# Row groups by one-row DMAs on SyncE, a hand-over awaited by TensorE, ranges of 46 nodes

## The reference, cut to what matters

```python
nodes = x[edges]                                   # source's and destination's state, side by side
gates = ssp(edge_attr @ We1 + be1) @ We2 + be2     # ssp is softplus less log 2
gates = gates * (1 - sigmoid(5 * (distance - 3.5)))
h = ssp(nodes @ Wn1 + bn1) @ Wn2 + bn2
sums = zeros_like(x).at[dst].add(h * gates)
new = x + ssp(sums @ Ws1 + bs1) @ Ws2 + bs2
out = layernorm(x + new)
```

## Time and profile before

| | us |
|---|---|
| median of three runs (1990.34 to 1991.43) | 1991.15 |
| the profiled execution | 1991.78 |
| its span, first to last instruction | 1989.6 |
| share of the span busy: TensorE, weight load, VectorE, ScalarE, GpSimd | 88%, 67%, 64%, 74%, 75% |

### The profile page before, as it was taken

The page is one execution under the profiler, slowest core; times in us unless marked ns, Lnnn a source line. Parts: engine busy times, 40 slices in busy tenths (PEclk is TensorE's granted clock), DMA queues, the critical chain, the costliest instruction groups (busy, mean ns, idle before and its releaser), DMA issues.

```text
span 1989.6 us, 52758 instructions
## 1 busy us (share of the span) xinstructions
PE 1744.9 (88%) x16249; PEld 1331.2 (67%) x16249; DVE 1281.8 (64%) x3512; ACT 1470.9 (74%) x2586; POOL 1483.8 (75%) x1572
## 2 busy tenths in 40 slices
PE   4699999989889888899888998888998898888897
PEld 3477777777667666666666776666776666666666
DVE  4577777766655655656566666666666666666666
ACT  2478888877776777767677777777777777777776
POOL 7777777777777777777777777777777777777773
PEclk7799999998998999989999999999989999999999
DMA  5433333333333333333333333333333333333331
GB/s 120 118 89 96 93 95 93 91 93 77 90 74 69 73 70 73 75 69 73 70 76 72 74 77 77 75 74 80 73 75 75 77 75 75 75 77 75 75 76 38
DMA packets 256432, 157.78 MB, mean 79 GB/s; under 512 B 45401, under 2 KB 227046, under 8 KB 256366
## 3 DMA queue, kind: packets, MB, share of 16 engines
q1 hardware_dynamic: 202652, 104.94, 18.1%
q0 software_dynamic: 50048, 51.35, 15.6%
q10 hardware_dynamic: 3666, 0.68, 0.2%
HBM read 146.94 MB, written 9.87 MB: 79 GB/s over the span
## 4 chain that ended last, share of the span: by engine, by line
POOL 55%; issue 20%; PE 14%; ACT 3%; DVE 2%; DMA 2%; SPq 2%; ACTq 1%; DVEq 0%; POOLq 0%
POOL ga L459 55%; PE ps L623 4%; PE ps L636 3%; PE ps L640 2%; PE ps L585 1%; PE ps L575 1%; DMA ga<-in_x_dram,srcT 1%; DVE hid L1114 1%; SPq L340 1%; ACT lg L865 1%; PE ps L653 1%; ACT lg L860 1%; PE ps L662 1%; PE ps L577 1%; DVE hid L1118 1%
## 5 line engine op out<-in xcount | busy, mean ns | idle before, releaser
L459 POOL DMA_INDIRECT ga<-in_x_dram,srcT x1564 | 1482.8, 948 | 477.7 <-issue 472.4
L852 ACT ACTIVATE lg<-ps,bn1c 128x512 f32<-128x512 f32 x391 | 268.6, 687 | 374.9 <-PE ps L585 351.7
L636 PE MATMUL ps<-wn,hid 128*128 128x64 f32 x3128 | 446.6, 287 | 35.7 <-DVE hid L1118 31.0
L1114 DVE SCALAR_TENSOR_TENSOR hid<-ps,neg_b,lg 128x512 f32<-128x512 f32 x391 | 293.0, 749 | 264.5 <-ACT lg L865 253.0
L636 PEld LDWEIGHTS ps<-wn,hid 128*128 128x128 f32 x3128 | 391.8, 197 | 71.6 <-DVE hid L1118 48.5
L860 ACT ACTIVATE lg<-lg 128x768 f32<-128x768 f32 x391 | 335.6, 858 | 0.0
L865 ACT ACTIVATE lg<-lg 128x768 f32<-128x768 f32 x391 | 332.2, 850 | 0.0
L575 PE MATMUL ps<-ident,ea 128*128 128x128 f32 x782 | 173.6, 305 | 174.2 <-DMA ga<-in_x_dram,srcT 117.6
L844 ACT COPY xe<-ps 128x512 f32<-128x512 f32 x391 | 230.0, 588 | 104.9 <-PE ps L577 92.0
L623 PE MATMUL ps<-xe,wn 64*128 64x256 f32 x1564 | 293.1, 453 | 0.0
L640 PE MATMUL ps<-we,hid 128*128 128x128 f32 x1564 | 274.5, 301 | 0.0
(11 more groups left out here) (122 smaller groups left out, 1526.3 us busy)
## 6 DMA issues: line engine op xcount, KB each, us to landing
ea<-in_edge_attr_dram SPq DMA_DIRECT2D x195, 256.0 KB
ga<-in_x_dram,srcT POOLq DMA_INDIRECT x1564
bw<-b_tab SPq DMA_DIRECT2D x782, 32.0 KB
relb<-rel_tab SPq DMA_DIRECT2D x196, 64.0 KB
b_tab<-share SPq DMA_DIRECT2D x25, 250.0 KB
out_dram<-xs SPq DMA_DIRECT2D x25, 125.0 KB
xs<-in_x_dram SPq DMA_DIRECT2D x3, 750.0 KB
rows_i<-in_dst_dram SPq DMA_DIRECT2D x1, 768.0 KB
```

The source lines that it names most:

```text
L459: pool.indirect_dma_start(to[:, t % 2, t // 2, :], None, x, bass.IndirectOffsetOnAxis(ap=idx[:, t:t + 1], axis=0)).then_inc(done, 16)
L636: pe.matmul(hg[:, t * D:(t + 1) * D], hid[:, u % 2, t * P:(t + 1) * P], wn2[:, :], start=False, stop=False, skip_group_check=True)
L852: act.activation(lg[:, u % 2, 0:QUAD].rearrange("p (k e) -> p k e", k=2), z[:, :, 0:PAIR], ACT.Abs, bias=bn1c[:, 0:1])
L1114: dve.scalar_tensor_tensor(out=hid[:, u % 2, 0:QUAD].rearrange("p (k e) -> p k e", k=2), in0=ps[:, 2 * (u % 2):2 * (u % 2) + 2, 0:PAIR], s ...
```

## The change

For 13 quads (80, 104, ... 368, every 24th) GpSimd issues three gathers instead of four, the third adding 32 to s_ga. The rows of t = 3 are fetched by SyncE with 128 DMAs of one row each into a buffer, stage (two row groups), and go from there into ga by one DMA of 128 rows. The one-row DMAs are spread over SyncE's steps from 30 quads before the quad to 8 before it, 12 or 8 a step (12 steps: 8 of 12, 4 of 8), so that from step 50 on to step 360 every step issues some; the copy into ga is issued in the step 4 quads before the quad. The places of the rows are read out of row_at, one partition of an old buffer, loaded at the start by a DMA of 13 x 128 numbers and multiplied by 256 on VectorE. TensorE, every 8th quad from 16 on, waits for the semaphore handed, which SyncE raises by 16 every 8 quads after 80, by the copy's completion where that quad is one of the 13; GpSimd waits for nothing new. W becomes 46, with the halves of the partitions still at 0 and 64 (HALF). A second table, wb_tab / wb_all, holds the ranges' places in bytes, so that SyncE need not multiply; SyncE reads them eight at a time, every 4 quads. SyncE's code is written out for all quads.

```diff
-W = 64
+HALF = 64
+W = 46
+ROWS0 = 80
+ROWS_EVERY = 24
+ROWS_N = 13
+ROWS_BEFORE = 30
+ROWS_TURN = (12, 8, 12, 12, 8, 12, 12, 8, 12, 12, 8, 12)
+HAND = 8
+ROWS_FIRST = tuple(sum(ROWS_TURN[:n]) for n in range(len(ROWS_TURN)))
...
+        stage = sb("stage", [P, 2, D])
...
-                    sp.dma_start(bw[n % 2 * W:(n % 2 + 1) * W, v + n // 2, :],
-                                 b_tab[bass.ds(first, W), :]).then_inc(s_bw[v], 16)
+                    sp.dma_start(bw[n % 2 * HALF:n % 2 * HALF + W, v + n // 2, :].bitcast(U8),
+                                 b_bytes[bass.ds(first, W * F * 4)].rearrange("(r b) -> r b", b=F * 4)).then_inc(s_bw[v], 16)
+
+            def load_rows(q):
+
+                i, turn = divmod(q - (ROWS0 - ROWS_BEFORE), ROWS_EVERY)
+                turn //= 2
+                if not (q >= ROWS0 - ROWS_BEFORE and i < ROWS_N):
+                    return
...
+                if i >= 2 and turn == 0:
+                    sp.wait_ge(xe_t, ROW_QUADS[i - 2] + 1)
+                first, n = ROWS_FIRST[turn], ROWS_TURN[turn]
+                _, places = nc.values_load_multi_w_load_instructions(
+                    row_at[:, i * P + first:i * P + first + n], engines=(mybir.EngineType.SP,), min_val=0,
+                    max_val=(N - 1) * D * 4, skip_runtime_bounds_check_because=IN_X)
+                for r, place in enumerate(places):
+                    sp.dma_start(stage[first + r:first + r + 1, i % 2, :].bitcast(U8),
+                                 x_bytes[bass.ds(place, D * 4)].rearrange("(r b) -> r b", r=1)).then_inc(s_stage[i % 2], 16)
+
+            def hand_rows(q):
+
+                i, off = divmod(q - (ROWS0 - 4), ROWS_EVERY)
+                if 0 <= i < ROWS_N and off == 0:
+                    quad = ROW_QUADS[i]
+                    sp.wait_ge(s_stage[i % 2], P * 16 * (i // 2 + 1))
+                    sp.wait_ge(xe_t, quad - (ARING - 1))
+                    sp.dma_start(ga[:, quad % ARING, 1, 1, :], stage[:, i % 2, :]).then_inc(handed, 16)
+                if q > ROWS0 and q % HAND == 0 and q not in ROW_QUADS:
+
+                    sp.sem_inc(handed, 16)
...
-                _, firsts = nc.values_load_multi_w_load_instructions(
-                    w_all[0:1, bass.ds(q * 2, 2 * n)], engines=(mybir.EngineType.SP,), min_val=0, max_val=N - W,
-                    skip_runtime_bounds_check_because=IN_RANGE)
+                if v % 4 == 0:
+                    m = min(4, NQ - q)
+                    _, starts[0:2 * m] = nc.values_load_multi_w_load_instructions(
+                        wb_all[0:1, bass.ds(q * 2, 2 * m)], engines=(mybir.EngineType.SP,), min_val=0, max_val=(N - W) * F * 4,
+                        skip_runtime_bounds_check_because=IN_RANGE)
+                firsts = starts[v % 4 * 2:v % 4 * 2 + 2 * n]
                 load_rel(q, u)
                 load_bw(q, v, firsts)
                 if reached(q, RING):
                     load_ea(q, u)
+                load_rows(q)
+                hand_rows(q)
...
+                sp.sem_inc(handed, (ROWS0 - ARING) // HAND * 16)
+                sp.wait_ge(row_e, XCOLS)
+                sp.dma_start(row_at.rearrange("p (i e) -> p i e", e=P),
+                             src[(ROWS0 + 1 - ROWS_EVERY) * QUAD:(ROW_QUADS[-1] + 1) * QUAD].rearrange(
+                                 "(a i e) -> a i e", a=1, e=ROWS_EVERY * QUAD)[:, :, (ROWS_EVERY - 1) * QUAD + PAIR + 1:ROWS_EVERY * QUAD:2]).then_inc(ld_row, 16)
                 for q in range(BRING):
                     fast_step(q, q)
...
-                gather_rows(ga[:, q % ARING], srcT[:, 4 * q:4 * q + 4], s_ga[q % ARING])
+                to, idx, done = ga[:, q % ARING], srcT[:, 4 * q:4 * q + 4], s_ga[q % ARING]
+                if q in ROW_QUADS:
+
+                    gather(to, idx, 0, done)
+                    gather(to, idx, 1, done)
+                    gather(to, idx, 2, done, 32)
+                else:
+                    gather_rows(to, idx, done)
...
                 pe.wait_ge(s_ga[v], per_ring(q, v, ARING, 64))
+                if v % HAND == 0 and reached(q, ARING):
+                    pe.wait_ge(handed, q * (16 // HAND) - (16 // HAND * ARING - 16))
...
                 four_steps(1, 1, 0, False, True)
+                dve.wait_ge(ld_row, 16)
+                dve.tensor_scalar(row_at, row_at, float(D * 4), None, ALU.mult).then_inc(row_ready, 1)
```

More of the change, by code:

```diff
@@ L25 @@
 BRING = 8
+ROWS0 = 80
[5 more added lines that the diff above has]
+ROWS_FIRST = tuple(sum(ROWS_TURN[:n]) for n in range(len(ROWS_TURN)))
 IN_RANGE = "windows' places are the least of N - W and of destinations, which are nodes"
+IN_X = "sources are nodes"
 def reached(i, n):
@@ L85, in gnn_layer @@
     assert RG > 1 and RL > 1
+    ROW_QUADS = [ROWS0 + ROWS_EVERY * i for i in range(ROWS_N)]
+    assert sum(ROWS_TURN) == P and all(n % 4 == 0 for n in ROWS_TURN) and 2 * len(ROWS_TURN) == ROWS_EVERY
+    assert ROWS0 % HAND == 0 and ROWS_EVERY % HAND == 0 and ROWS0 >= ROWS_EVERY and ROW_QUADS[-1] < NQ - 4
     STEPS = 8
@@ L201, in gnn_layer @@
         dst_i = rows_d[:, :, :].rearrange("p g e -> p (g e)")[:, 0:NT].bitcast(I32)
+        row_at = rows_i[0:1, :, :, :].rearrange("p a g e -> p (a g e)")[:, 0:ROWS_N * P]
         gen_flat = sb("gen_flat", [P, 10 * P])
@@ L260, in gnn_layer @@
         g_oh, g_mm, g_add = ([sem(f"{n}{k}") for k in range(2)] for n in ("g_oh", "g_mm", "g_add"))
+        ld_row, row_ready, wb_ready, wb_stored = (sem(n) for n in ("ld_row", "row_ready", "wb_ready", "wb_stored"))
+        handed = sem("handed")
+        s_stage = [sem(f"s_stage{k}") for k in range(2)]
         filled, hg_set = sem("filled"), sem("hg_set")
@@ L414, in _ @@
                     load_x(n)
-                for q in range(BRING, 2 * BRING):
-                    fast_step(q, q % BRING)
[L419 to L441, removed]
+                ahead = NODE0 + STEPS
+                for q in range(BRING, NQ):
+                    stored, made, node = (q - 12) // 4, (q - 7) // 4, (q - (ahead + STEPS - 1)) // STEPS
+                    if q % 4 == 0 and 1 <= stored < NG:
+                        share_stored(stored // 2, stored % 2)
+                    fast_step(q, q % BRING)
+                    if q % 4 == 3 and SHARES <= made < NG:
+                        store_share(made, made % 2)
+                    if q % STEPS == (ahead - 1) % STEPS and 0 <= node < EARLY:
+                        store(node)
             for g in range(EARLY, NG):
@@ L454, in _, with gather @@
             pool.iota(iota_pi[:, :], pattern=[[1, 1]], base=0, channel_multiplier=1).then_inc(iotas, 1)
+            def gather(to, idx, t, done, inc=16):
+                pool.indirect_dma_start(to[:, t % 2, t // 2, :], None, x,
+                                        bass.IndirectOffsetOnAxis(ap=idx[:, t:t + 1], axis=0)).then_inc(done, inc)
             def gather_rows(to, idx, done):
                 for t in range(4):
-                    pool.indirect_dma_start(to[:, t % 2, t // 2, :], None, x,
-                                            bass.IndirectOffsetOnAxis(ap=idx[:, t:t + 1], axis=0)).then_inc(done, 16)
+                    gather(to, idx, t, done)
             def fast_step(q):
@@ L621, in front @@
                         half = slice(k * D, (k + 1) * D)
-                        weights, rows = (wn1[half, 0, :], xe[half, u, 1, :]) if end == 0 else (bw[half, b, :], ohT[half, u % 2, :])
+                        near = slice(k * HALF, k * HALF + W)
+                        weights, rows = (wn1[half, 0, :], xe[half, u, 1, :]) if end == 0 else (bw[near, b, :], ohT[near, u % 2, :])
                         pe.matmul(ps[:, 2 * (u % 2) + k, 0:PAIR], weights, rows,
```

22 lines of the change are left out of this document (18 added, 4 removed).

## The result

| | before | changed |
|---|---|---|
| median of five runs, us | 1991.15 (1990.33 to 1991.83) | 1979.99 (1978.92 to 1983.78) |
| the profiled execution | 1991.78 | 1978.96 |
| its span | 1989.6 | 1977.2 |
| end of the last gather in it | 1962.2 | 1948.5 |
| from there to the end of the span | 27.4 | 28.7 |

The changed kernel takes 0.9946 of the time before (95%: 0.9935 to 0.9957): 11.2 us less, where the prediction had 16. The sign and the mechanism are the forecast ones, the size is not: the time lies within the range given (1969 to 2030), but just above the forecast's own one (1970 to 1979). It falls where the prediction had put "in part" (1979 to 1987, a chance of 0.08).

A forecast was written before the change was run, and what follows sets the result against it. GpSimd's gathers bound the kernel: -16.3 us for 13 fewer, +0.3 for the added 32, so -16.0, with up to 0.5 either way for the tail, gives 1975 us from 1991.15. Range 1969 to 2030, the forecast's own 1970 to 1979.

The forecast's parts named there:

- in part: Rival: 12-row steps in a row make SyncE late now and then, 0.05 us a step: 1983 us, chance 0.08.
- Bound and gain: GpSimd sets the time; 13 gathers fewer at 1.251 us each save 16.3 us.
- in the shade of GpSimd: W = 46 shortens the last quads' one-hot and scatter by under 0.5 us; elsewhere its gain is hidden behind GpSimd.
- The sum of 9.4 us: SyncE's work per step of two quads after the change, fitting under GpSimd's 9.90 us with 0.5 us to spare.
- (c): SyncE's bw DMAs of 46 rows: 0.33 us an issue, four times -0.14, so -0.56 us a step.
- (e: SyncE's new one-row DMAs, 10.67 a step at 0.40 us each: 4.3 us a step (3.7 to 6.9).
- (f): SyncE's load of 8 or 12 places for the one-row DMAs: 1.05 us, up to 2.5 at VectorE's rate.
- (d): SyncE loads eight places every second step, 0.75 us, for four every step: -0.10 us a step.
- The rival of the crowded DMA engines: Rival: bw rows fall on two DMA engines and loads land later; 2170 us at 50 ns a packet, chance 0.04.
- SyncE the bound: Rival: SyncE's step exceeds 9.93 us in 156 steps; 2068 or 2209 us, range 2000 to 2250, chance 0.20.
- Too late or the same: Rival: each of the 13 quads waits for its hand-over as long as a gather; 1991 us, chance 0.06.
- Start and hand-over: Start delays the compute 2 to 6 us, made up by the tenth quad; TensorE's wait for handed: both cost 0.

The follow-up runs named there:

- no_rows: Changed kernel with GpSimd gathering all four groups of every quad and SyncE fetching no rows, W = 46 kept: 1.0033 of the kernel before, 1997.25 us.
- three_gathers: As no_rows, but the 13 quads take three gathers and nothing fetches their fourth row group: 0.9950 of the kernel before, 1981.50 us.
- no_rows_w64: Changed kernel without SyncE's rows, GpSimd gathering everything, and with W = 64: 1.0004 of the kernel before, 1992.41 us.
- w64: Changed kernel with its rows and W = 64 instead of 46: 0.9929 of the kernel before, 1978.14 us.
- before_w46: Kernel before with W = 46 instead of 64 as its only change: 1.0019 of the kernel before, 1994.46 us.
- w48: Changed kernel with W = 48 instead of 46, nothing else: 0.9938 of the kernel before, 1979.79 us.
- rel16: Changed kernel, W = 46, with relb loaded by two DMAs of 64 rows each instead of one: 0.9956 of the kernel before, 1983.41 us.
- every16_w64: Changed kernel with W = 64 and 19 quads, every 16th, 16 one-row DMAs in each of SyncE's steps: 1.0915 of the kernel before, 2178.68 us.
- pool_waits: Changed kernel with GpSimd, not TensorE, waiting for handed, ahead of the third gather of the 13 quads: 1.0039 of the kernel before, 1997.88 us.

## Why the prediction was right, and by what it was off

**Bound and gain.** GpSimd is the bound and a gather is worth its full period: right. 15.8 us between no_rows and three_gathers, 14.3 between no_rows_w64 and w64, 17.3 between no_rows and the changed kernel, for 16.3.

The range held the result easily, but its width up to 2030 was there for the slower cases, which didn't come. In the prediction the stretch from 1979 to 1987 belongs to a SyncE that is late now and then; three_gathers, which has no such rows and is no faster, speaks against that reason. What put the time there was the following.

**The failed step is W = 46.** I let its effect beyond the tail lie "in the shade of GpSimd". A shorter instruction there does lie in the shade, but what came was a loss that the sum had no term for, together with twice the time at half clock. By the ratios that term is +3.8 us on the kernel before (before_w46), +5.8 on the one without rows (no_rows and no_rows_w64; +4.8 by the medians) and +1.6 to +3.4 on the changed one, where the intervals overlap. So it accounts for a third to some two thirds of the 5 us between 1975 and 1980. w64, which doesn't pay it, is still 2 to 3 us above the forecast; its last gather ends at 1950.6, where 16.3 us less than before would be 1945.9, and its gathers take 951.0 ns on the mean for 948.1. In the profiled execution of the changed kernel 1.3 us of the difference lie in the tail, for which I had allowed 0.5 either way, and 2.6 in a slower gather, part of which is scatter. Why the gathers are slower stays open.

How the half clock comes about is seen only in part. 21 of the 23 stretches in the changed kernel begin in a pause of TensorE of over 1 us, as that of 2.33 us above, or at most 2.2 us behind its end, and so do all 29 in the kernel before. But a pause alone is not enough: the kernel before has 76 of them after 130 us, the changed one 32. There are no more falls than before, 23 for 29. They last longer, 12.8 us on the mean for 5.7; why, these runs don't show.

**SyncE's step.** The sum of 9.4 us was too high by the prices: a step of 12 rows takes 7.9, or 8.3 with half a load of eight places, where my terms give 10.0. bw 0.256 us for 0.33 (c), a one-row DMA 0.228 and 0.35 with what lies between for 0.40 (e: (4.07 - 0.23)/11; the 0.05 that I had added for a register address is not there, 0.228 with one against 0.238 without), the load of 12 places 0.937 for 1.05 (f), of eight 0.786 for 0.75 (d). The rival's prices, VectorE's 0.23 us a register, did not come: on SyncE it is 0.08 with twelve. The Trainium skill, "Runtime: NRT & Kernel Launch", section "Instruction fetch mechanics", gives about 200 ns a register, by my estimate 2.4 us for twelve. The row disagrees; the figure of the Trainium skill is for registers loaded from HBM, while these places lie in SBUF.

And yet SyncE has less room than that suggests. Between 284 and 530 us its steps are 10.0 us apart with 6 us of waits in all, since issues are held up where shares are stored as well; and at 590 us a late ea lies on the chain. The issues in question, then the piece of the chain, then the same issue in w64:

```profile
593.44 0.55 SPq L351 DMA_DIRECT2D relb<-rel_tab  x1
594.11 1.49 SPq L360 DMA_DIRECT2D bw<-b_tab  x4
595.64 1.28 SPq L343 DMA_DIRECT2D ea<-in_edge_attr_dram  x1
```

```profile
595.64 7.11 DMA ea<-in_edge_attr_dram
```

```profile
598.68 0.58 SPq L343 DMA_DIRECT2D ea<-in_edge_attr_dram  x1
```

ea takes 1.28 us to issue and 7.11 to land, where 256 KB took 3.3 before. TensorE's pause of 2.33 us lasts until that landing, and the 37.5 us at half clock begin in it. I had named a landing of 6 us or more as a sign against the forecast, and TensorE waiting for ea as another. Both came, the first in half of all loads (6.0 us at the median) and the second with 50.3 us, and the direction held all the same: w48 and rel16 take the waits away and gain nothing. They were poor signs.

**The rival of the crowded DMA engines** (called the third in one place of the prediction, the second in its list) was right in mechanism and wrong in weight. 46 rows do fall on two engines, and the gathers' packets take longer: the share of queue 0 rose from 15.6% to 19.5% over the whole run, though there are fewer gathers, and to 18.8% in 1000 to 1100 us by the narrower loads alone (before_w46). The Trainium skill, "DMA: Bandwidth & Descriptors", section "Why a DMA increments its semaphore by 16 and not by 1", says that the number of engines divides the rows; the traces agree (2.95 semaphore events for 46 rows, 14.6 for 48 and 13.6 for 64). No step is decided by it at this traffic: w48 and rel16, which take the crowding away, are no faster.

**SyncE the bound** is right as a mechanism beyond its point, as every16_w64 shows (11.1 us a step, 2179); the change lies below that point. **Too late or the same** lives in pool_waits, 1998, though by two waits and not by 13. **Start and hand-over** at nothing: right. no_rows_w64, which has the start's DMA and product and the waits for handed, is level with before, and three_gathers has neither fetch nor copy and is no faster than the changed kernel.

**The signs.** Last gather starting near 1945: 1947.5. One-row issues of 0.25 to 0.35 us: 0.23. SyncE's waits of 0.3 to 0.6 us a step: 0.24 between 284 and 530 us, 1.2 from there to 1807. 23 and then 20 quads in 100 us: 22, then 19, the latter at a granted clock of 0.83.

## What to carry to other kernels

An operand that is made smaller in the shade of the bound is not free of charge: look at the granted clock and at the number of DMA engines that the new shape gets, and time that edit alone on the old kernel (here +3.8 us). Work moved to an idle queue is free while the queue keeps a reserve in the stretch where it is fullest, and the mean over the run doesn't show that stretch. Let the wait for a hand-over stand on the engine that arrives last, not on the bound that runs ahead. Of the versions here the one with W = 64 came out fastest (0.9929) and scattered least, though its lead over the changed kernel is at the edge of what these runs tell apart.

## What the runs showed of the hardware that I had not expected

- The longest half-clock stretch is 34.1 to 51.2 us in the traces with W = 46 and 34.1 with W = 48; with W = 64 none outlasted 13.7 us, apart from every16_w64 (23.9). A quad takes 7.15 us in one and 3.95 at full clock.
- The price of issuing a load went with the parts that it lands in and with the rows: 0.256 us for 46 rows (2 parts), 0.372 for 48 (16 parts), 0.545 for 64 (16 parts). Where the view was not in bytes it was less, 0.238 for 46 rows (before_w46) and 0.469 for 64 (before).
- Loading registers on SyncE takes 0.332 us for two places, 0.477 for four, 0.786 for eight, 0.937 for twelve and 1.166 for sixteen.
- With 46-row loads and relb on two engines each, the gathers' packets took longer: their share rose by a quarter (15.2 to 18.9% in 1000 to 1100 us, for 2560 and 2559 packets), was 15.5% with 48 rows, and fell to 14.0% when only relb was spread wider. ea's landing, 3.0 us at the median before, took 6.0, then 3.0 (w48) and 4.2 (rel16).
